# A graph network's edge sort: the rank of an edge counted by ScalarE's running sum of signs instead of VectorE's compares

## The reference

```
h   = relu(x @ Wp.T + bp)
agg = segment_sum(h[src], dst, N) / max(count of edges into the row, 1)
x   = agg @ Wl.T + bl + x @ Wr.T
```

## Time and profile before

| | |
|---|---|
| median of 3 runs | 1545.38 us (1542.32 to 1546.3) |
| the profiled execution | 1550.21 us, of which its span is 1548.5 us |
| TensorE busy | 98% of the span |
| VectorE, ScalarE, GpSimd busy | 63%, 44%, 38% |
| node phase of layer 0 | about the first 255 us |
| ranks | 40, starting between 36.5 and 176.7 us |

### The profile page before, as it was taken

How to read it: one execution, slowest core, us unless ns; L and a number is a source line. 1 busy time by engine, 2 the same in 40 slices (tenths; PEclk the granted TensorE clock), 3 DMA queues, 4 the chain that set the end, 5 groups by cost and what they waited for, 6 DMA issues and landing times.

```text
span 1548.5 us, 21498 instructions
## 1 busy us (share of the span) xinstructions
PE 1513.7 (98%) x7355; PEld 1235.9 (80%) x7355; DVE 979.9 (63%) x2156; ACT 688.1 (44%) x1267; POOL 583.2 (38%) x534
## 2 busy tenths in 40 slices
PE   7998999999999999999999999999999999999997
PEld 5777887888888788888788888878888887788886
DVE  7999874755555576767475555557577674655552
ACT  5544452332323576776332323347566662323322
POOL 4838743444423100200334442323354465444323
PEclk9999999999999999999999999999999999999999
DMA  8896786555553778877654554479899986454434
GB/s 295 326 370 214 247 271 207 127 88 90 89 93 52 217 265 275 279 272 265 194 127 89 89 92 85 58 233 321 295 329 325 323 296 200 77 93 86 79 42 60
DMA packets 152856, 291.74 MB, mean 188 GB/s; under 512 B 19885, under 2 KB 19948, under 8 KB 152620
## 3 DMA queue, kind: packets, MB, share of 16 engines
q1 hardware_dynamic: 123708, 224.81, 42.0%
q0 software_dynamic: 28464, 64.51, 23.7%
q10 hardware_dynamic: 576, 1.05, 0.2%
HBM read 132.33 MB, written 157.92 MB: 187 GB/s over the span
## 4 chain that ended last, share of the span: by engine, by line
PE 88%; DVE 5%; DMA 3%; issue 2%; ACT 1%; another core or an unknown queue 0%; SPq 0%; POOL 0%; POOLq 0%; DVEq 0%; ACTq 0%
PE bank L728 12%; PE bank L729 12%; PE bank L730 12%; PE bank L716 9%; PE bank L839 7%; PE bank L841 7%; PE bank L840 7%; PE bank L818 7%; PE bank L820 7%; PE bank L819 7%; DMA node_x<-xn 3%; DVE rows_out L1098 1%; DVE stats L1068 1%; DVE h_low L1042 1%; PE bank L790 1%
## 5 line engine op out<-in xcount | busy, mean ns | idle before, releaser
L728 PE MATMUL bank<-w_high,h_low 128*128 128x512 f32 x900 | 377.4, 419 | 0.0
L729 PE MATMUL bank<-w_low,h_high 128*128 128x512 f32 x900 | 358.5, 398 | 0.0
L730 PE MATMUL bank<-w_high,h_high 128*128 128x512 f32 x900 | 356.7, 396 | 0.0
L976 ACT ACTIVATE h_high<-h_pre 128x500 fp32r<-128x500 f32 x120 | 74.6, 622 | 448.0 <-DVE h_pre L1266 445.9
L585 POOL DMA_INDIRECT rows_in<-node_x,sorted_src x120 | 120.8, 1007 | 288.4 <-PE bank L716 201.8
L922 ACT ACTIVATE h_high<-bank 128x512 fp32r<-128x512 f32 x221 | 131.5, 595 | 170.8 <-PE bank L716 164.8
L730 PEld LDWEIGHTS bank<-w_high,h_high 128*128 128x128 f32 x900 | 170.7, 190 | 40.8
L1045 DVE TENSOR_TENSOR h_low<-bank,h_high 128x512 fp32r<-128x512 f32 x152 | 105.0, 691 | 147.9 <-ACT h_high L922 141.9
L818 PE MATMUL bank<-xt_low,w_high 128*128 128x500 f32 x480 | 194.7, 406 | 2.4 <-DVE h_pre L1257 2.0
L956 ACT ACTIVATE xn<-rows_in,off,rstd 128x512 f32<-128x512 f32 x237 | 189.4, 806 | 15.5 <-issue 12.9
L728 PEld LDWEIGHTS bank<-w_high,h_low 128*128 128x128 f32 x900 | 171.6, 191 | 30.8
(11 more groups left out here) (126 smaller groups left out, 2238.3 us busy)
## 6 DMA issues: line engine op xcount, KB each, us to landing
node_x<-xn SPq DMA_DIRECT2D x237, 256.0 KB
rows_in<-node_z SPq DMA_DIRECT2D x158, 256.0 KB
node_z<-rows_out SPq DMA_DIRECT2D x142, 256.0 KB
out<-rows_out SPq DMA_DIRECT2D x79, 256.0 KB
rows_in<-x SPq DMA_DIRECT2D x78, 256.0 KB
residual<-x SPq DMA_DIRECT2D x78, 256.0 KB, 4.3
node_z<-bias_z SPq DMA_DIRECT2D x16, 256.0 KB
rows_in<-node_x SPq DMA_DIRECT2D x16, 256.0 KB, 2.6
```

What stands on the lines that cost most here:

```text
L728: nc.tensor.matmul(psum, low[:, k, :], w_high("r", l)[:, k, :], start=(k == 0), stop=False)
L729: nc.tensor.matmul(psum, high[:, k, :], w_low("r", l)[:, k, :], start=False, stop=False)
L730: last = nc.tensor.matmul(psum, high[:, k, :], w_high("r", l)[:, k, :], start=False, stop=(k == K - 1))
```

## The change

The count of smaller keys is made on ScalarE. `Sign(key - other)` is 1 for a smaller key, -1 for a larger one and 0 for the key itself; ScalarE sums it over the 500 keys, and the count is half of (sum + 499). VectorE makes that last step for 8 tiles at once, in one new instruction at the head of `rows_of`, which the following ones wait for. The rank keeps its place in the steps, but stands in ScalarE's loop, behind `xn` and ahead of the weights' high parts.

```diff
@@ tiles and semaphores
+        above = sb("above", [P, EDGE_TILES], F32)
+        places_done = sem("places_done")
@@ ScalarE
+            def rank(t):
+                g = t // GROUP
+                if t == 0:
+                    act.wait_ge(digits, 5)
+                else:
+                    act.wait_ge(placed, t)
+                act.wait_ge(row_loaded[t // (EDGE_TILES // ROW_CHUNKS)], DMA)
+                S.activation(unused[0:EDGE_ROWS, :],
+                             key_row[0:EDGE_ROWS, g * GROUP:(g + 1) * GROUP, :].rearrange("p a e -> p (a e)"),
+                             ACT.Sign, bias=key_f[0:EDGE_ROWS, t:t + 1], scale=-1.0,
+                             accum_out=above[0:EDGE_ROWS, t:t + 1]).then_inc(placed, 1)
...
                         node_norm(l, u)
                     if l == 0 and -K <= i < 0:
                         high_r(0, i + K)
+                    if l == 0 and 0 <= i - STEP_RANK < EDGE_TILES:
+                        rank(i - STEP_RANK)
                     if 0 <= i - STEP_SPLIT_P < K:
                         high_p(l, i - STEP_SPLIT_P)
@@ VectorE
-            def rank(t):
...
-                V.scalar_tensor_tensor(out=unused[0:EDGE_ROWS, :].rearrange("p (a e) -> p a e", a=GROUP),
-                                       in0=key_row[0:EDGE_ROWS, g * GROUP:(g + 1) * GROUP, :],
-                                       scalar=key_f[0:EDGE_ROWS, t:t + 1],
-                                       in1=ones[0:EDGE_ROWS, 0:EDGE_ROWS].rearrange("p (a e) -> p a e", a=1)
-                                       .to_broadcast([EDGE_ROWS, GROUP, EDGE_ROWS]), op0=ALU.is_lt, op1=ALU.mult,
-                                       accum_out=place[0:EDGE_ROWS, t:t + 1]).then_inc(placed, 1)
-
             def rows_of(b):
...
                 dve.wait_ge(placed, (b + 1) * SPREAD)
+                V.tensor_scalar(of, above[0:EDGE_ROWS, cols], 0.5, (GROUP_ROWS - 1) / 2, ALU.mult, ALU.add
+                                ).then_inc(places_done, 1)
+                dve.wait_ge(places_done, b + 1)
...
-                    if l == 0 and 0 <= i - STEP_RANK < EDGE_TILES:
-                        rank(i - STEP_RANK)
```

## The result

| | median of 4 runs | range |
|---|---|---|
| before | 1545.84 us | 1542.32 to 1546.34 |
| after | 1529.61 us | 1528.88 to 1532.54 |

The profiled execution of after took 1528.88 us, with a span of 1527.1.

The account below looks back on a forecast made before the run. The prediction took TensorE, busy 98% of the span, as the bound, so only its waits and clock could be won: 2.8 + 2.4 + 0.2 + 0.3 = 5.7 us, 1545.4 to 1539.7 us; own range 1537.9 to 1541.4.

Parts of the forecast that it names:

- the stall of `off`: Beside GpSimd's four subtractions, `off` would stand 3.3 us, until 144.7; TensorE's 3.79 us wait falls to 1.0, winning 2.8.
- the wait of 1.77 us: TensorE's wait for the count digits near 110 us, behind a late store: mostly stays, about 0.2 us won.
- the forecast's start of 1545.4: The median time of the kernel before, from which the saving of 5.7 us was subtracted.
- wide range: The range of 8 in 10 for the measured time, from 1535.8 (full gain and spread) to 1545.5 us (no gain).
- The clock, 2.38 us: TensorE's lower clock behind the 3.79 us wait, at 140 to 150 us: would return in full, winning 2.38 us.
- the small wait, 0.3: The last small wait of TensorE at L781: VectorE's spare time covers it, winning 0.3 us.
- rival 2: Both waits go, as ScalarE's rank is short (0.62) and `off` misses most subtractions: 8.2 us won, 1537.2; chance 0.14.
- ScalarE's ranks, cost 0: 40 ranks of 0.85 us, 34 us in all, fit into ScalarE's 65 us idle and cost TensorE nothing.
- Rival 3: ScalarE becomes the bound once a rank exceeds 1.77 us, through table loads each step: 61 us more, 1606; chance 0.06.
- The 1.8, 3.8 and 2.4 us: TensorE's losses before: the count-digit wait, the wait behind the stalled rank, and the lower clock after it; 7.9 us offered.

Follow-up runs that it names:

- h3: The kernel before, unaltered, profiled a third time on a chip that ran every kernel some 8 us slower: 1550.66 us.
- e1: The kernel before with the new 160-byte tile added but unused, no instruction changed: ratio 0.9987 to before.
- e3: The kernel before with only ranks 30 and 31, beside GpSimd's four subtractions, moved to ScalarE: ratio 0.9995 to before.
- g3: A separate kernel: 48 times GpSimd makes a mask and four subtractions while VectorE starts a compare or `off` at shifted moments; no kernel time given.
- e8: The kernel before with ranks 0 to 21 moved to ScalarE and the other 18 left on VectorE: ratio 0.9979 to before.
- e4: The kernel before without any rank, each edge's place made from its position: 1532.97 us, ratio 0.9942 to before.
- e6: The changed kernel with each of ScalarE's Sign passes issued twice: 1535.95 us, ratio 0.9956 to before.
- e2: The changed kernel without the new tile, the sums going into `place`: 1533.61 us, ratio 0.9948 to before.
- h1: The changed kernel without the new tile, run again beside the changed kernel on a slower chip: 1543.21 us, ratio 0.9949 to before.
- h2: The changed kernel once more, tile included, on the same slower chip: 1540.26 us, ratio 0.9933 to before.
- e7: The kernel before with GpSimd's four subtractions made one at a time, four masks apart, ranks still on VectorE: ratio 0.9995 to before.

## Why the prediction was wrong

**The forecast's size.** It said 5.7 us; the repeated comparisons give about 10.4. Its mechanism (VectorE relieved, waits and clock won back, ScalarE for nothing) was right in direction. The steps that failed are the stall of `off` (1.0 us of wait), the wait of 1.77 us that was to stay, and the shift by the extra tile, which it didn't have. Even 10.4 us, 1535.0 from the forecast's start of 1545.4, lies just outside its wide range, which began at 1535.8; no rival had a sum that large.

- **`off` stands until 144.7, 1.0 us of wait is left: wrong.** It stood 0.70 us and nothing was left. The prediction took over from the stalled rank that a blocked instruction stays blocked until the series is over; the row that it gave for `off`, at most 1.269 us, is one instruction of GpSimd and not four. In after and in its variants without rank on VectorE `off` was let in at the next boundary; the longer holds, of a rank (before, h3, e1) or of `off` (e3), all came with VectorE late, but the second execution of before was late too and had none. The Trainium skill's rule (SBUF — State Buffer, "Who interferes with whom") says that the one that issues first has the shared pair for the whole instruction. All 48 turns of g3 agree with it, and so does after (0.70 us); a stall of 5.5 us over four instructions is more than the rule gives, and why it came is open. 1.0 us too little.
- **The wait of 1.77 us stays: wrong, and the bigger lesson.** I priced the ranks behind the store wait and took the store wait itself (5.18 us) as given. With the ranks gone it fell to 2.16 us, and the wait for the digits to nothing. That it was VectorE's load in the steps ahead is shown by e8 (2.19 us) and e4 (2.26), and e6 has the reverse: a ScalarE with steps of 3.26 us brings 3.61 and 1.82 us back. 1.6 us too little.
- **The clock, 2.38 us: right** in that it came back in full, though no wait was left on which its reason (a wait of 1.0 us leaves the clock alone) could be tried; **the small wait, 0.3: right.** With the two above the waits and the clock are 3.79 + 1.77 + 0.28 + 2.38 = 8.2 us, and e2 and h1 measure 8.0 and 7.9 by their ratios (9.2 and 7.45 by the medians). That is the figure of rival 2, but not by its reasons: the rank took 0.79 us and not 0.62, and `off` did meet the subtractions.
- **The extra tile: missed.** No step of the prediction asked what a tile of 160 bytes moves. It is worth 2 to 3 us (h1 and h2), and its cause is open.
- **ScalarE's ranks, cost 0: right** (0.79 us for 0.85; e4). Rival 3's point of 1.77 us a rank was not reached by any run; at 1.58 (e6) ScalarE already costs 3.8 us, by waits.
- **The starting point.** The 1.8, 3.8 and 2.4 us were taken as fixed properties of the kernel before. They are those of one execution: others show 2.9 + 0.5, or 1.4 + 4.0, against the prediction's word that the saving is "a matter of order and not of the execution". That the sum of the first execution, 8.2 us, meets the measured 8.0 is partly luck, since the three lose 3.4 to 5.9 us at L781 and have node phases of 234.9 to 238.4. What they share is a VectorE nearly as slow as TensorE's step, and e7, which takes away the stall alone, and e3, which shortens it, win nothing that can be told from zero.

**The rest of the first comparison** (16.2 us, interval 11.9 to 17.9) is explained only in part. Its two profiles differ by 4 us more at one place behind 1290 us, where the kernel before waited in layer 2:

```profile
PE bank L818 <- DVE h_pre L1257: 2.0, 1, 2.0
...
PE bank L839 <- DVE h_low L1272: 1.0, 1, 1.0
```

After has none of these in its first profile, but the changed kernel without the tile has both on the slower chip (h1: 2.0 and 1.0 us), and after has 3.2 us there (h2). They come with the change and without it, so they aren't the change's. The later comparisons, with 21 and 9 runs of before and 6 and 5 of after, give 0.9937 and 0.9933, whose intervals touch the first one's end; I take 10.4 us (9.7 and 10.4 by the ratios).

## What to carry to other kernels

A single long wait in a profile is often only the place where an engine's general lateness comes out; compare that engine's work per step with the step of the engine that bounds the kernel first, and if the two are within a few per cent (here 3.25 and 3.45 us), relieve it everywhere rather than at the wait. A wait for a store may belong to whoever made the stores late, so don't hold it fixed when that engine is relieved. An added tile is a change of its own and needs its own control (here e2 and h1). And profile the kernel before twice before pricing its waits one by one.

## What the runs showed of the hardware that was not expected

- A VectorE instruction with two SBUF inputs was held over several back-to-back instructions of GpSimd in some executions (5.52, 5.54, 6.01, 3.16 us), and let in at the next boundary in others (0.70 us in after, at most 1.724 us for a compare in g3), with the same code (the ranks in the three executions of before: 5.52, at most 0.93, 5.54). In all four long holds GpSimd was already at work when VectorE's instruction started, in before and e1 with the mask ahead of the subtractions; what no run explains is why VectorE then got no turn at the two to four boundaries that followed. In h3, VectorE and then GpSimd:

```profile
138.61 5.54 DVE L1138 SCALAR_TENSOR_TENSOR unused<-key_row,key_f,ones 125x500 bf16<-125x500 f32 x1
```

```profile
138.49 4.98 POOL L578 TENSOR_TENSOR w_low<-stage,w_high 128x512 fp32r<-128x512 f32 x4
```

- A compare that gets its turn holds GpSimd in the same way: GpSimd's next subtraction took 1.70 us in place of 1.26 in g3.
- Where tiles lie in SBUF, with the program otherwise the same, changes the distance between TensorE's matmuls: 3.2134 to 3.2335 us a step of 16 instructions, 0.6%.
- ScalarE's reading of a sum is 0.189 us, where VectorE's is 0.080, and ScalarE ran Sign, Relu, Identity and Sqrt in turn on one table load.
